# Two Fourier layers on one core: the layer-0 products of the last stage as pairs of 64-row tiles instead of a block-diagonal matrix of 128 rows

## What is computed

```
x = x + conv0(gn(x))       # spectral: 16 x 16 low modes, one 64 x 64 matrix per mode; skip: v @ skip_kernel + skip_bias
x = x + conv1(gn(x))       # spectral: 32 x 32 modes at both ends of the first axis; out = irfft2(...)
                           # relu(out @ W + b + out)
```

## Time and profile before

| what | value |
|---|---|
| median of three runs | 2296.1 us (2288.66 to 2303.97) |
| profiled execution: span from the first to the last instruction | 2287.4 us |
| TensorE matmul busy | 1824.6 us, 80% of the span, 24234 instructions |
| VectorE busy | 1462.2 us, 64% |
| ScalarE busy | 1128.0 us, 49% |
| GpSimd busy | 263.8 us, 12% |
| HBM | 240 GB/s over the span |

### The profile page before, as it was taken

How to read it: one execution, slowest core, us unless ns; L and a number is a source line. 1 busy time by engine, 2 the same in 40 slices (tenths; PEclk the granted TensorE clock), 3 DMA queues, 4 the chain that set the end, 5 groups by cost and what they waited for, 6 DMA issues and landing times. The chain is left out here.

```text
span 2287.4 us, 57711 instructions
## 1 busy us (share of the span) xinstructions
PE 1824.6 (80%) x24234; PEld 1460.3 (64%) x24234; DVE 1462.2 (64%) x2219; ACT 1128.0 (49%) x1852; POOL 263.8 (12%) x476
## 2 busy tenths in 40 slices
PE   5899989998197433332564999999989999999999
PEld 3677767677155333332553788787868878787887
DVE  5876777773447211112563788787868878787887
ACT  5765556662043000000333677676656767666665
POOL 0000000000102100000252110303021030303000
PEclk9999999999555556655876999999999999999999
DMA  8887887881965999996744888888887888888886
GB/s 302 311 262 239 260 267 255 264 270 23 219 77 110 265 253 284 254 264 172 237 150 133 295 282 289 305 311 321 298 299 271 284 321 296 320 311 319 296 293 261
DMA packets 240450, 585.68 MB, mean 256 GB/s; under 512 B 71170, under 2 KB 160770, under 8 KB 203906
## 3 DMA queue, kind: packets, MB, share of 16 engines
q1 hardware_dynamic: 163778, 515.47, 68.9%
q10 hardware_dynamic: 71040, 60.70, 10.4%
q0 software_dynamic: 5376, 5.76, 0.9%
HBM read 381.01 MB, written 168.30 MB: 240 GB/s over the span
## 5 line engine op out<-in xcount | busy, mean ns | idle before, releaser
L1298 ACT ACTIVATE x_turned<-ps_xt 128x512 f16<-128x512 f32 x512 | 305.6, 597 | 333.2 <-PE ps_xt L1384 333.2
L1428 PE MATMUL ps_y<-apply,x_turned 128*128 128x128 f16 x6144 | 428.5, 220 | 0.0
L1340 DVE TENSOR_TENSOR x_turned<-ps_xt,x_turned 128x512 f16<-128x512 f32 x512 | 351.2, 686 | 106.9 <-ACT x_turned L1298 106.9
L1428 PEld LDWEIGHTS ps_y<-apply,x_turned 128*128 128x128 f16 x6144 | 377.9, 98 | 64.8 <-issue 1.1
L221 DVE TENSOR_TENSOR parts<-stage,parts 128x1024 f16<-128x1024 f32 x256 | 301.9, 1220 | 107.7 <-ACT parts L145 107.1
L1361 DVE SCALAR_TENSOR_TENSOR y_out<-ps_y,relu 128x512 f32<-128x512 f32 x512 | 351.3, 686 | 22.6 <-PE ps_y L1428 4.1
L1384 PE MATMUL ps_xt<-c_eye,x_in 128*128 128x128 f32 x2048 | 312.2, 275 | 22.1 <-DMA x_in<-in_x 22.1
L1308 ACT ACTIVATE relu<-ps_wave 128x512 f32<-128x512 f32 x512 | 303.2, 592 | 13.8 <-PE ps_wave L1414 13.8
L145 ACT ACTIVATE parts<-stage 128x1024 f16<-128x1024 f32 x256 | 255.1, 1049 | 76.3 <-issue 40.7
L1332 DVE SCALAR_TENSOR_TENSOR low_tile<-ps_col,high_tile 128x512 f16<-128x512 f32 x256 | 176.6, 691 | 115.8 <-ACT high_tile L1292 115.8
L290 PE MATMUL row_ps<-parts,c_rows_dft 128*64 128x512 f16 x1536 | 200.6, 389 | 61.5 <-DVE parts L221 53.8
(11 more groups left out here) (121 smaller groups left out, 1978.7 us busy)
## 6 DMA issues: line engine op xcount, KB each, us to landing
stage<-in_x SPq DMA_DIRECT2D x256, 512.0 KB, 4.7
x_in<-in_x SPq DMA_DIRECT2D x128, 1024.0 KB, 9.6
out_y<-y_out SPq DMA_DIRECT2D x128, 1024.0 KB, 6.0
fw_first<-in_fw SPq DMA_DIRECT2D x9, 2048.0 KB, 19.5
fw<-in_fw ACTq DMA_DIRECT2D x8, 2048.0 KB, 22.8
fw<-in_fw SPq DMA_DIRECT2D x8, 2048.0 KB, 20.3
fw_first<-in_fw ACTq DMA_DIRECT2D x7, 2048.0 KB, 20.8
raw<-mixed ACTq DMA_DIRECT2D x12, 1024.0 KB, 7.4
```

What stands on the lines that cost most here:

```text
L1298: nc.scalar.activation(turned[u % 2][:, 0, :, :], ps_turn[u % 2][:, :, :], ACT.Copy).then_inc(turn_high, 1)
L1340: nc.vector.tensor_tensor(v[:, 1, :, :], ps_turn[u % 2][:, :, :], v[:, 0, :, :], ALU.subtract).then_inc(turn_split, 1)
L1428: mm = nc.tensor.matmul(ps_y[u % 2][:, :, 2 * k:2 * k + 2], turned[u % 2][:, p, k, :], apply[:, bass.ds(b, 1), q, :, :].rearrange("p o c w ...
```

## The change

`apply` loses its zeros and its last axis: rows (e, c), 64 columns c'. Each product is split into two, for e = 0 and e = 1, on the rows 0 to 63 and 64 to 127 of x_turned, both with 128 weight columns and 64 data columns, and the two write to different PSUM banks (ps_y{i}_{e}), as contiguous runs of 64. ps_y therefore takes four banks instead of two; ps_col and ps_wave keep one each, with waits that are one group and one unit tighter. The layer-0 wave matmul and the y instruction are split in two by e. The GpSimd memsets of `apply` go, and VectorE makes it with two instructions instead of four.

```diff
-            for d, other in ((slice(0, C), 1), (slice(C, P), 0)):
-                nc.gpsimd.memset(apply[d, :, :, :, other], 0.0).then_inc(zeroed, 1)
-            pool.wait_ge(zeroed, 3)
...
-            for j, d in enumerate(halves):
-                ins = nc.vector.tensor_scalar(apply[d, :, 0, :, j], A[d, :, :], 16.0, None, ALU.mult)
-            step(ins)
-            for j, d in enumerate(halves):
-                nc.vector.scalar_tensor_tensor(out=apply[d, :, 1, :, j], in0=A[d, :, :], scalar=16.0,
-                                               in1=apply[d, :, 0, :, j], op0=ALU.mult,
-                                               op1=ALU.subtract).then_inc(apply_ready, 1)
+            step(nc.vector.tensor_scalar(apply[:, :, 0, :], A[:, :, :], 16.0, None, ALU.mult))
+            nc.vector.scalar_tensor_tensor(out=apply[:, :, 1, :], in0=A[:, :, :], scalar=16.0, in1=apply[:, :, 0, :],
+                                           op0=ALU.mult, op1=ALU.subtract).then_inc(apply_ready, 1)
...
-        ps_col = [m.ps(f"ps_col{i}", [P, WB // UW, GC, UW]) for i in range(2)]
+        ps_col = m.ps("ps_col", [P, WB // UW, GC, UW])
...
-        ps_y = [m.ps(f"ps_y{i}", [P, C, UW]) for i in range(2)]
-        ps_wave = [m.ps(f"ps_wave{i}", [P, C, UW]) for i in range(2)]
+        ps_y = [[m.ps(f"ps_y{i}_{e}", [P, 512]) for e in range(2)] for i in range(2)]
+        ps_wave = m.ps("ps_wave", [P, C, UW])
...
+        def y_bank(u, e):
+
+            return ps_y[u % 2][e][:, 0:UW // 2 * C].rearrange("p (k c) -> p k c", c=C)
...
-                    nc.vector.scalar_tensor_tensor(out=y_out[ch % Y_SLOTS][:, j * UW:(j + 1) * UW, :],
-                                                   in0=ps_y[u % 2][:, :, :].rearrange("p c w -> p w c"), scalar=1 / 16,
-                                                   in1=relu[u % 2][:, :, :],
-                                                   op0=ALU.mult, op1=ALU.add).then_inc(y_done, 1)
+                    for e in range(2):
+                        done = nc.vector.scalar_tensor_tensor(out=y_out[ch % Y_SLOTS][:, j * UW + e:(j + 1) * UW:2, :],
+                                                              in0=y_bank(u, e), scalar=1 / 16,
+                                                              in1=relu[u % 2][:, e::2, :], op0=ALU.mult, op1=ALU.add)
+                    done.then_inc(y_done, 1)
...
-                pe.wait_ge(col_taken, group_number(b, t, g) + 1)
+                pe.wait_ge(col_taken, group_number(b, t, g) + 2)
...
-                    pe.wait_ge(relu_ready, b * U + u + 1)
+                    pe.wait_ge(relu_ready, b * U + u + 2)
...
                     pe.wait_ge(y_done, b * U + u + 1)
-                    nc.tensor.matmul(ps_y[u % 2][:, :, :], w["waves_h0"][:, hh, :], zero, start=True, stop=False)
+                    for e in range(2):
+                        nc.tensor.matmul(y_bank(u, e).rearrange("p k c -> p c k"), w["waves_h0"][:, hh, :],
+                                         zero[:, :, e::2], start=True, stop=False)
...
                     for k in range(UW // 2):
                         for n, (p, q) in enumerate(((0, 0), (0, 1), (1, 0))):
-                            mm = nc.tensor.matmul(
-                                ps_y[u % 2][:, :, 2 * k:2 * k + 2], turned[u % 2][:, p, k, :],
-                                apply[:, bass.ds(b, 1), q, :, :].rearrange("p o c w -> p (o c) w"),
-                                start=False, stop=(n == 2 and k == UW // 2 - 1))
+                            for e in range(2):
+                                half = slice(e * C, (e + 1) * C)
+                                mm = nc.tensor.matmul(y_bank(u, e)[:, k, :], turned[u % 2][half, p, k, :],
+                                                      apply[half, b, q, :], start=False,
+                                                      stop=(n == 2 and k == UW // 2 - 1))
                     mm.then_inc(y_ready, 1)
...
-        apply = m.sb("apply", [P, B, 2, C, 2], F16)
+        apply = m.sb("apply", [P, B, 2, C], F16)
```

More of the change, by code:

```diff
@@ L606, in _ @@
             dve.sem_inc(input_ready, 1)
-            halves = [slice(0, C), slice(C, P)]
-            for j, d in enumerate(halves):
-                ins = nc.vector.tensor_scalar(apply[d, :, 0, :, j], A[d, :, :], 16.0, None, ALU.mult)
-            step(ins)
-            for j, d in enumerate(halves):
-                nc.vector.scalar_tensor_tensor(out=apply[d, :, 1, :, j], in0=A[d, :, :], scalar=16.0,
-                                               in1=apply[d, :, 0, :, j], op0=ALU.mult,
-                                               op1=ALU.subtract).then_inc(apply_ready, 1)
+            step(nc.vector.tensor_scalar(apply[:, :, 0, :], A[:, :, :], 16.0, None, ALU.mult))
+            nc.vector.scalar_tensor_tensor(out=apply[:, :, 1, :], in0=A[:, :, :], scalar=16.0, in1=apply[:, :, 0, :],
+                                           op0=ALU.mult, op1=ALU.subtract).then_inc(apply_ready, 1)
             dve.wait_ge(GA_ready, 1)
@@ L698, in apply_to_modes @@
                 if t == 0:
-                    pe.wait_ge(apply_ready, 2)
+                    pe.wait_ge(apply_ready, 1)
                 if t >= 2:
@@ L703, in apply_to_modes @@
                 for n, (p, q) in enumerate(((0, 0), (0, 1), (1, 0))):
-                    last = nc.tensor.matmul(ps_apply[t % 2][0:C, :], apply[0:C, b, q, :, 0], xm_parts[t % 2][:, p, :],
+                    last = nc.tensor.matmul(ps_apply[t % 2][0:C, :], apply[0:C, b, q, :], xm_parts[t % 2][:, p, :],
                                             start=(n == 0), stop=(n == 2))
@@ L1274, in column_bank @@
         def column_bank(g):
-            return ps_col[g % 2][:, :, :, :].rearrange("p k c w -> p k (c w)")
+            return ps_col[:, :, :, :].rearrange("p k c w -> p k (c w)")
+        def y_bank(u, e):
+            return ps_y[u % 2][e][:, 0:UW // 2 * C].rearrange("p (k c) -> p k c", c=C)
         @block.gpsimd
@@ L1307, in image @@
                     act.wait_ge(y_done, b * U + u + 1)
-                    nc.scalar.activation(relu[u % 2][:, :, :], ps_wave[u % 2][:, :, :].rearrange("p c w -> p w c"), ACT.Relu,
+                    nc.scalar.activation(relu[u % 2][:, :, :], ps_wave[:, :, :].rearrange("p c w -> p w c"), ACT.Relu,
                                          scale=1 / 16).then_inc(relu_ready, 1)
@@ L1394, in columns @@
                     for q in range(2):
-                        last = nc.tensor.matmul(ps_col[g % 2][:, :, c, :], by_channel[:, g * GC + c, :],
+                        last = nc.tensor.matmul(ps_col[:, :, c, :], by_channel[:, g * GC + c, :],
                                                 w["waves_w"][:, q, t * WB:(t + 1) * WB], start=(q == 0), stop=(q == 1))
@@ L1411, in image @@
                         pe.wait_ge(tiles_filled, 16 * COPIES * (b * BLOCKS + t + 1))
-                    pe.wait_ge(relu_ready, b * U + u + 1)
+                    pe.wait_ge(relu_ready, b * U + u + 2)
                     for q, v in enumerate((high, low)):
-                        mm = nc.tensor.matmul(ps_wave[u % 2][:, :, :], w["waves_h1"][:, hh, q, :], v,
+                        mm = nc.tensor.matmul(ps_wave[:, :, :], w["waves_h1"][:, hh, q, :], v,
                                               start=(q == 0), stop=(q == 1))
```

## The result

The changed kernel takes 2368.8 us (median of three, 2363.95 to 2374.59) against 2296.1: a ratio of 1.031 (95% interval 1.027 to 1.036), 3.1% slower. Predicted were 2340 us, slower, with a range of 2272 to 2510.

The account below looks back on a forecast made before the run. TensorE was taken to bound pass_2, with x_in transfers as reserve. Units +41, start +19, norm_0 -1 and x_in waits -15 made +44 us: 2331 of span, 2340 beside the median after adding 8.7; range 2272 to 2510.

Parts of the forecast that it names:

- TensorE bounds, with the transfers as its reserve: In pass_2 TensorE time is kernel time; longer units shrink the 22.1 us of waits for x_in by 15 us.
- The products: L1428: 24 half-size matmuls overlapping in pairs take 0.34 us instead of 0.67, gaining 0.33 us per unit.
- Rival B: At L1428 pairs bring nothing, products stay at 0.67 us; 2502 us, or 2389 with single writes free; chance 0.29.
- Rival C: At L1428 the 64-row loads lose the quick form or exclude each other, products take 1.34 us; 2845 us; chance 0.08.
- The switch of shape: TensorE changing between 128-row and 64-row tiles twice per unit costs 0.10 and 0.09, together 0.19 us per unit.
- The layer-0 matmul: L1418, split into two of 256 columns writing single PSUM elements, takes double the time: +0.22 us per unit.
- Rival A: At L1418 single writes run at full rate, costing 0 instead of 0.22 us; not slower, 2280 us; chance 0.20.
- The sum of the unit: TensorE's unit in pass_2 gets 0.08 us longer, plain units 1.84 us; 512 units give +41 us.
- One bank each: Single banks for ps_wave and ps_col cost nothing within the loop, but +19 us in the 16 groups ahead of it.
- Rival D: The ring of matmuls, ScalarE and VectorE on one ps_col bank binds: 0.2 us in 240 units, 2388 us; chance 0.07.
- VectorE's y: One 512-element instruction of 0.69 us becomes two of 0.42: +0.15 us per unit, hidden by TensorE.
- norm_0: Two pairs of VectorE instructions become one of each, -1.2 us on a path where TensorE waits; counted as -1.

Follow-up runs that it names:

- the best version: Changed kernel with channel-innermost wave tiles, two banks in turn for column groups ahead of the loop, and ps_wave(u) ahead of turn(u+1): 2270.0 us, ratio 0.9875.
- the three fastest versions with 24 products per unit: Changed kernel with channel-innermost tiles, 2300.2 us; also with two banks in turn ahead of the loop, 2286.1; also with ps_wave(u) ahead of turn(u+1), 2270.0.

## Why the prediction was right, and by what it fell short

Direction, bound and mechanism held; the gain per unit was smaller and one cost larger than the sum had them, 0.15 us per unit instead of 0.08. The range, 238 us wide, made the number easy to meet; the likeliest case's own band, 2325 to 2360, ended 9 us too low.

- *TensorE bounds, with the transfers as its reserve.* Held. +76 us of units showed as +79.4 of the stage, together with the start and the waits. The waits lost 16.5 us; I had put 15.
- *The products.* 0.34 forecast, 12 pairs of 0.030 are 0.36, a gain of 0.31 instead of 0.33. The nearest row, the column pairs of L306, held for row pairs. Rival B fell: four instructions per 30 ns are issued. Rival C fell: the loads keep their 95 ns record.
- *The switch of shape.* This is the mis-sized term: 0.19 forecast, 0.25 measured. 0.10 in (0.53 less twice 0.216), 0.09 to 0.10 back, and 0.05 in the transposes behind it. The sign "0.15 to 0.2 at the first transpose" was off: the first starts 0.12 us after the last product, the second one 0.165 after the first. I had taken L318's own spacing of 0.12 as its rhythm; the same tiles stand 0.11 apart in pass_2, so the late second transpose was in that mean and I took it off as rhythm (the first two L318 of the earlier trace rows start 0.164 apart, the others 0.109).
- *The layer-0 matmul.* +0.22 forecast, +0.216 to 0.22 measured, shown by putting it in (2373 us, unit +0.22) and taking it out (-69 us, unit -0.21). The sign named for it, the two starts 0.21 apart, was not quite met: they lie 0.178 apart, and the rest comes behind the second. Rival A fell. The prediction laid the cost to single writes and did not see that the reads go from 2 to 4 bytes apart with them; no run changed the writes alone, so the cost is shown and its reason is argued. The trace agrees with the rule that the prediction cited from the Trainium skill, Advanced Engine Details and Errata, section Memory Cachelines, that every two consecutive elements should be contiguous: L1428 writes pairs at 0.056 us for 128 columns, and the matmuls with single fp32 take twice the time.
- *The sum of the unit.* -0.33 + 0.19 + 0.22 = 0.08 against -0.31 + 0.25 + 0.22 = 0.16, measured 0.15. 512 x 0.07 = 36 us is nearly the whole miss in the stage (+79.4 against +45). That the median missed by 29 us only is chance: the 8.7 us added for the median beside the profiled execution did not come back, since the changed kernel's median lies below its profiled span.
- *One bank each.* +19 forecast, +20 in the profile, shown both ways (medians +15 and -20.4); nothing in the loop, as forecast. Rival D fell.
- *VectorE's y.* 0.417 us each, forecast 0.42, hidden. *norm_0:* the two instructions take 1.1 us where the four took 2.4, as forecast; in the time this is lost in the scatter ahead of pass_2.
- *The floor of about 25 ns between starts* that the prediction cited from the Trainium skill, page TensorE: Matmul & The Clock Gate, section "Wait — 56ns, not 53.3ns?", does not hold across two tiles: 24 products took 0.36 us, not 0.60. In the trace the two of a pair start 3 to 4 ns apart. Within one tile they came 0.029 apart.

## What to carry to other kernels

Halving an operand to use both halves of the array pays only what remains after the way in and out of that shape, here 0.25 us per visit, so gather much work per visit; behind it an f16 matmul was 0.045 us better than an fp32 transpose. Before splitting an accumulation over banks, walk through the order of every matmul that writes it, on both sides: here single fp32 results with every second f16 read cost double, neighbouring results with one f16 read per 16 bytes cost four times, and a layout change upstream freed both. And when a bank is taken from a double buffer, look for the stretch with nothing beside it, not for the steady loop. Count the instructions too: halved products are twice as many, and in the best version that cost 38 us of waits.

## What the runs showed of the hardware that was not expected

- Two matmuls of 256 columns that read one f16 out of every 16 bytes started 0.43 us apart, four times the 0.11 of neighbours.
- A matmul that writes single fp32 values and reads every second f16 costs double, 0.216 us for 256, whatever the distance of the writes (8 or 256 bytes), and the cost can appear later: the second start comes after 0.178 and the rest in the matmuls behind. Which of the two it is was not separated.
- Products on the second half of the rows overlap earlier ones on the first even when not interleaved: the first three of 12 started before the last of the other 12.
- TensorE can run out of instructions. In the three fastest versions with 24 products per unit it stood for 24, 31 and 38 us in pass_2, always at the same place in a block of 256 of its instructions, give or take one, and until 0.9 to 1.7 us after a 16 KB packet of the instruction queue had landed. A packet took 1.0 us in the median, in the kernel before as in these, so it is the number of blocks, 144 instead of 92 in one stage, that differs.
